# VectorE takes unit 3 between the gram products of the two batches, and the output's sums of squares behind the first two units' products

## The chip, the cores and the metric

One Trainium2 chip, one core of it. The core has TensorE (PE in the profile, PEld its weight loads), VectorE (DVE), ScalarE (ACT), GpSimd (POOL) and SyncE (SP, which only issues DMAs here). The metric is the device time in microseconds of one execution; the median of several runs is quoted. The profile is of one execution and is a little off the median.

## The reference, cut to what matters

Two sequences of 4096 rows of 512 values go through a layer norm; the result feeds two branches, whose outputs are both added to the input.

```python
xn = layernorm(x)
x  = x + attn(xn) + ffn(xn)

# attn: gated delta rule, 16 heads, keys of 16, values of 32
q, k, v = silu(causal_conv4(xn @ W))
S = S * exp(g);  delta = (v - k S) * beta;  S = S + k delta;  o = q S      # per row
o = o * rsqrt(mean(o * o over the 32 values of a head) + eps)              # sums of squares
o = o * silu(gate);  attn = o @ o_w.T

# ffn: 4-bit weights, 1408 inner columns
h = silu(xn @ gate_w.T) * (xn @ up_w.T);  y = h @ down_w.T;  ffn = y / rms(y)
```

## The kernel before, in words

The 4096 rows are taken in 32 tiles of 128 rows, both batches together (`NB = 2`). The kernel is written by hand, engine by engine: each engine has one step function (`sp_step`, `pool_step`, `act_step`, `dve_step`, `pe_step`), whose order of calls is the order of its queue, and every dependence is a wait on a semaphore. A step has two tiles: `t`, the previous one, whose attention is finished in this step, and `n`, the present one, whose projections, convolution, decay matrices, gram matrices and whole feed-forward part are made in it. There are 33 steps: the first has no `t`, the last no `n`, and 31 have both.

What the steps of the prediction touch:

- **Units.** The feed-forward part makes 22 units, `unit(0)` to `unit(21)`: even ones are a 128-column slice of gate, odd ones of up. PE makes four partial products in two halves (`half_unit`, lines 1127 to 1155), ACT copies the first one scaled into `fa` (line 613), and DVE adds the other three with their scales (`unit`, line 893). ACT takes the silu of a gate (`gate(m)`, line 624), and DVE multiplies it with the up slice (`hidden(m)`, line 905). `fa` has four slots, so ACT's copy of unit 5 waits for `hidden(1)`. PE's `down(m)` (line 1166) uses the hidden slices, and PE's units wait for earlier units of DVE to give their PSUM back.
- **Gram products.** PE makes the gram matrices of one batch (`gram(b)`, line 1354) in four PSUM banks; DVE multiplies them with the decay matrix (`gram_products(b)`, lines 987 and 988), one result going to DRAM through SP (lines 391 to 400) as the matrix that POOL solves, the other staying as `D`. The gram of batch 1 uses the same banks, so it waits for the products of batch 0. PE's transposes of v (line 1469) and its unit 5 wait for the products of batch 1.
- **The output's norm.** For the previous tile, ACT copies the output out of PSUM and squares it into `osq` (line 776), DVE sums the squares by head into `so` (line 1049), POOL makes the scale from them (lines 535 and 538, a power) and multiplies the gated output with it (`gated_and_scaled`, line 543), one instruction a batch. PE transposes the scaled output (`turn_o`, line 1366, behind unit 8), ACT copies it, and PE multiplies it with the output weights (`to_wo`, line 1376).
- **The solve.** POOL's next work, `solve` (lines 494 to 515), inverts a 32 x 32 triangle per head by 62 instructions; it first clears its result (lines 501 and 503) and waits for the DMA that brings the matrix. SP writes the result to DRAM and reads it back turned (lines 411 and 417), and PE's `t_times_r` (line 1221) uses it in the next step.

PE's order around the change is:

```python
unit(2); gram(0); unit(3); gram(1); unit(4)
# transposes of v, both batches
unit(5); unit(6); unit(7); down(0)
# then unit(8), turn_o, unit(9), down(1), unit(10), to_wo(0, 0), ...
```

Of the kernel before, what the change touches and what calls it, by code (L numbers as in the profile page):

```python
# [91 lines left out]
def build(nc, A, out):  # L92
# [4 lines left out]
    with ExitStack() as ctx:  # L97
# [258 lines left out]
        def bank(u, fill):  # L356

            return (6 if u in (1, 3) else 2 if u % 2 else 4) + fill
# [506 lines left out]
        def dve_step(eng, t, n, more):  # L865
# [15 lines left out]
            def unit(u):  # L881

                if not n:
                    return
                m = u // 2
                eng.wait_ge(*fa_scaled.at(n, u + 1))
                for k in range(1, KB):
                    if k == 2:
                        eng.wait_ge(*gu_out.at(n, 2 * u + 2))
                        eng.wait_ge(*fa_second.at(n, u + 1))  # L890
                    elif k == 3:
                        eng.wait_ge(*fa_third.at(n, u + 1))
                    eng.scalar_tensor_tensor(out=fa[:, u % 4, :], in0=PS[:, bank(u, k // 2), k % 2 * NB * P:][:, 0:NB * P],  # L893
                                             scalar=sc[:, u % 2, KB * m + k:KB * m + k + 1], in1=fa[:, u % 4, :],
                                             op0=ALU.mult, op1=ALU.add).then_inc(
                        (fa_second, fa_third, fa_done)[k - 1].sem, 1)

            def hidden(m):
                if not n:
                    return  # L900
                eng.wait_ge(*sg_done.at(n, m + 1))
                eng.wait_ge(*fa_done.at(n, 2 * m + 2))
                if m == 0:
                    eng.wait_ge(*halo_out.at(n, 1))
                eng.tensor_tensor(inner[:, m, :], fa[:, (2 * m + 1) % 4, :], sg[:, m % 2, :], ALU.mult).then_inc(h_done.sem, 1)  # L905
# [69 lines left out]
            def gram_products(b):  # L975
                if not n:
                    return
                eng.wait_ge(*gram_out.at(n, b + 1))
                eng.wait_ge(*decay_done.at(n, b + 1))

                def heads(ap):
                    return ap.rearrange("p (f g e i) -> p g f (e i)", f=NHALF, g=4, e=2)

                Gq = PS[:, 0:4, 0:4 * CH].rearrange("p g (f n) -> p g f n", f=NHALF)
                Gk = PS[:, 0:4, 4 * CH:8 * CH].rearrange("p g (f n) -> p g f n", f=NHALF)
                Eb = E[:, b, :, :].rearrange("p h i -> p (h i)")
                eng.tensor_tensor(heads(kbq[:, b, :]), Gk, heads(Eb), ALU.mult).then_inc(a_done.sem, 1)
                eng.tensor_tensor(heads(D[:, b, :, :].rearrange("p h i -> p (h i)")), Gq, heads(Eb),  # L988
                                  ALU.mult).then_inc(p_done.sem, 1)
# [53 lines left out]
            unit(1)  # L1043
            unit(2)
            gram_products(0)
            if t:
                for b in range(NB):
                    eng.wait_ge(*osq_done.at(t, b + 1))
                    eng.tensor_reduce(so[:, b, :], osq[:, b, :].rearrange("p (h v) -> p h v", v=DV), AX.X,
                                      ALU.add).then_inc(so_done.sem, 1)  # L1050
            gram_products(1)
            unit(3)
            hidden(0)
            hidden(1)
            if not n:
                result(0)
                result(1)
# [16 lines left out]
        @block.vector  # L1074
        def _(eng):
            eng.memset(eps[:, :], 1e-6).then_inc(zeroed.sem, 1)
            eng.memset(mhalf[:, :, :], -0.5).then_inc(zeroed.sem, 1)
            eng.memset(halo[:, :, :, :], 0.0).then_inc(zeroed.sem, 1)
            eng.memset(S[:, :, :, :, :], 0.0).then_inc(zeroed.sem, 1)
            first = Tile(0, 0, first=True)  # L1080
            layer_norm_stats(eng, first)
            layer_norm_apply(eng, first)
            eng.wait_ge(first_loaded.sem, 16 * 2)
            eng.wait_ge(gup_loaded.sem, 32)
            for i in range(2):
                decode(eng, i)
            eng.wait_ge(consts_loaded.sem, 16 * 11)
            eng.tensor_copy(identb[:, :], ident[:, :]).then_inc(consts_done.sem, 1)
            eng.tensor_copy(laterR[:, :], later[:, :]).then_inc(consts_done.sem, 1)
            eng.tensor_tensor(biasS[:, :], bias[:, 0, :], bias[:, 1, :], ALU.add).then_inc(consts_done.sem, 1)  # L1090
            eng.tensor_scalar(negm[:, :], tri[:, :], 1.0, 30000.0, ALU.subtract, ALU.mult).then_inc(consts_done.sem, 1)
            eng.wait_ge(alog_exp.sem, 1)
            eng.tensor_scalar(negA[:, :], negA[:, :], -1.0, None, ALU.mult).then_inc(consts_done.sem, 1)
            eng.tensor_scalar(sc[:, 0, :], sc16[:, 0, :], F8_UNIT, None, ALU.mult).then_inc(consts_done.sem, 1)
            eng.tensor_scalar(sc[:, 1, :], sc16[:, 1, :], F8_UNIT * F8_UNIT, None, ALU.mult).then_inc(consts_done.sem, 1)
            for i in range(2, KB):
                decode(eng, i)
            eng.wait_ge(dnp_loaded.sem, 32)
            for i in range(KB, len(strips)):
                decode(eng, i)  # L1100
            run(eng, dve_step)
# [458 lines left out]
```

## Time and profile before

| | |
|---|---|
| median of 3 runs | 3336.32 us (3335.82 to 3341.81) |
| the profiled execution | 3332.51 us, its span 3330.7 us |
| TensorE clock granted | 0.988 of full speed on average |
| busy share | PE 94%, DVE 72%, POOL 58%, ACT 50% |
| instructions | 118645 |

The profile's page gives busy times of engines over the span, the chain of work that ended last, and the costliest groups of instructions by source line. A timeline lists one engine's instructions in order, merged where the same line follows itself; a bracket behind a row is idle time of that engine just before it, with what ended it. All rows of timelines below are from one tile in the middle of the loop, but for those of the last tile.

### The profile page before, as it was taken

Reading aid. Unit: us, or ns where it says so; the run is one execution under the profiler, and the core shown is the slowest. Engines: PE = TensorE matmul, PEld = TensorE weight load, DVE = VectorE, ACT = ScalarE, POOL = GpSimd, SP = SyncE. Lnnn points to the kernel's source line nnn. Section 1 sums busy time; section 2 is a strip of 40 time slices with the busy share of each in tenths; the row PEclk is TensorE's granted clock in tenths of the full one; section 3 lists DMA queues with packets and bytes.
Section 4 is the critical chain, followed back from the end, with each engine's and each line's share of the span. In section 5 each row is a group of like instructions: output and inputs, shape, how many; then the busy total and the mean of one; then the engine's idle time right before and its main releaser. Section 6 shows DMA issues by size and latency. Waiting matters only on the chain.

```text
span 3330.7 us, 118645 instructions
## 1 busy us (share of the span) xinstructions
PE 3142.1 (94%) x45632; PEld 2252.9 (68%) x45632; DVE 2390.6 (72%) x5408; ACT 1667.4 (50%) x3306; POOL 1918.8 (58%) x2865
## 2 busy tenths in 40 slices
PE   5999999999999999999999999999999999999995
PEld 4666766766666766666767767667667666767663
DVE  7677776777776777777777767777767777767772
ACT  3544554544554545554445545445545455544452
POOL 4566555666555665556665556665556655556652
PEclk8999999999999999999999999999999999999996
DMA  3111111111111111111111111111111111111111
GB/s 112 39 46 27 37 43 33 46 45 28 34 43 36 46 37 27 43 37 42 46 27 37 43 33 46 46 27 37 43 33 46 40 28 39 42 37 46 34 25 30
DMA packets 318318, 132.08 MB, mean 40 GB/s; under 512 B 277089, under 2 KB 278881, under 8 KB 317793
## 3 DMA queue, kind: packets, MB, share of 16 engines
q1 hardware_dynamic: 313824, 119.26, 14.3%
q8 instruction: 383, 6.28, 0.8%
q10 hardware_dynamic: 4096, 6.42, 0.5%
q14 instruction: 15, 0.11, 0.0%
HBM read 75.30 MB, written 50.33 MB: 38 GB/s over the span
## 4 chain that ended last, share of the span: by engine, by line
PE 77%; DVE 12%; issue 6%; POOL 2%; ACT 1%; ACTq 1%; DMA 1%; DVEq 0%; SPq 0%; POOLq 0%
PE PS L1166 17%; PE PS L1122 13%; PE PS L1153 8%; PE PS L1235 7%; PE PS L1154 7%; PE PS L1376 6%; DVE arena L893 4%; PE PS L1221 3%; PE PS L1300 2%; PE PS L1253 2%; DVE arena L378 2%; PE PS L1271 2%; PE PS L1391 2%; DVE arena L988 1%; PE PS L1178 1%
## 5 line engine op out<-in xcount | busy, mean ns | idle before, releaser
L893 DVE SCALAR_TENSOR_TENSOR arena<-PS,sc,arena 128x256 f32<-128x256 f32 x2112 | 1001.0, 482 | 253.0 <-ACT arena L613 152.2
L1153 PE MATMUL PS<-xh,wgu 128*128 128x256 f32 x2816 | 871.6, 341 | 35.9 <-DVE arena L893 35.4
L613 ACT ACTIVATE arena<-PS,sc 128x256 f32<-128x256 f32 x704 | 330.0, 474 | 759.0 <-PE PS L1154 700.3
L1154 PE MATMUL PS<-xl,wgu 128*128 128x256 f32 x2816 | 698.8, 282 | 0.0
L1166 PE MATMUL PS<-wdn,inner 128*128 128x512 f32 x1408 | 650.7, 592 | 0.0
L1153 PEld LDWEIGHTS PS<-xh,wgu 128*128 128x128 f32 x2816 | 531.2, 189 | 155.8 <-issue 84.2
L511 POOL TENSOR_TENSOR work<-arena 128x31 f32<-128x31 f32 (+15 forms) x992 | 511.9, 516 | 137.5 <-DMA arena<-scr_a 62.3
L515 POOL TENSOR_TENSOR arena<-arena,work 128x31 f32<-128x31 f32 (+15 forms) x992 | 542.1, 546 | 77.7
L1154 PEld LDWEIGHTS PS<-xl,wgu 128*128 128x128 f32 x2816 | 530.4, 188 | 83.2 <-issue 83.2
L1122 PE MATMUL PS<-xnT,wqkv 128*128 128x256 f32 x2048 | 485.6, 388 | 25.2 <-ACT inner L593 15.4
L1122 PEld LDWEIGHTS PS<-xnT,wqkv 128*128 128x128 f32 x2048 | 383.6, 192 | 93.1 <-ACT inner L593 16.4
L877 DVE SCALAR_TENSOR_TENSOR qkv<-inner,cw,qkv 128x256 f32<-128x256 f32 x768 | 398.8, 557 | 55.9 <-ACT qkv L600 46.7
L1166 PEld LDWEIGHTS PS<-wdn,inner 128*128 128x128 f32 x1408 | 245.5, 189 | 199.8 <-issue 199.4
L1235 PE MATMUL PS<-wg,xnT 128*128 128x512 f32 x512 | 264.8, 621 | 0.0
L1376 PE MATMUL PS<-wo,arena 128*128 128x512 f32 x512 | 242.0, 596 | 0.0
L378 POOL TENSOR_TENSOR R<-arena,ckg 128x256 f32<-128x256 f32 x64 | 57.3, 913 | 314.1 <-DVE ckt L959 314.1
L632 ACT ACTIVATE ub<-PS 32x512 f32<-32x512 f32 x256 | 136.7, 580 | 202.2 <-PE PS L1253 197.6
L905 DVE TENSOR_TENSOR inner<-arena,sg 128x256 f32<-128x256 f32 x352 | 203.4, 585 | 30.5 <-DVE arena L893 0.5
L624 ACT ACTIVATE sg<-arena 128x256 f32<-128x256 f32 x352 | 145.2, 413 | 154.1 <-DVE arena L893 153.8
L915 DVE TENSOR_TENSOR tmp<-PS,bdmask 128x128 f32<-128x128 f32 x256 | 74.1, 289 | 206.2 <-PE PS L1271 201.8
L533 POOL TENSOR_TENSOR arena<-arena 128x512 f32<-128x512 f32 x64 | 80.4, 1278 | 226.3 <-ACT qkv L776 226.3
L1071 DVE SCALAR_TENSOR_TENSOR obuf<-PS,yr,obuf 128x512 f32<-128x512 f32 x64 | 45.1, 745 | 217.6 <-POOL yr L527 217.6
(147 smaller groups left out, 4619.2 us busy)
## 6 DMA issues: line engine op xcount, KB each, us to landing
xt<-in_x SPq DMA_DIRECT2D x64, 256.0 KB, 2.8
scr_a<-arena SPq DMA_DIRECT2D x64, 256.0 KB, 2.4
arena<-scr_a SPq DMA_DIRECT2D x256, 64.0 KB, 3.2
obuf<-in_x SPq DMA_DIRECT2D x64, 256.0 KB, 2.8
scr_t<-arena SPq DMA_DIRECT2D x32, 512.0 KB, 2.7
arena<-scr_t SPq DMA_DIRECT2D x256, 64.0 KB, 2.3
out<-obuf SPq DMA_DIRECT2D x64, 256.0 KB, 2.0
wqkv<-in_wqkv ACTq DMA_DIRECT2D x1, 2048.0 KB, 14.3
```

The lines of the kernel that those rows point to most:

```text
L511: eng.tensor_tensor(pr, la[:, j, j + 1:].unsqueeze(1).broadcast_to([P, w, r]), bc(lt[:, 0:w, j], r), ALU.mult).then_inc(solve_part.sem, 1)
L515: eng.tensor_tensor(tail, tail, pr, ALU.subtract).then_inc((t_done if j == CH - 2 else solve_part).sem, 1)
L613: eng.activation(fa[:, u % 4, :], PS[:, bank(u, 0), 0:NB * P], ACT.Copy, scale=sc[:, u % 2, KB * m:KB * m + 1]).then_inc(fa_scaled.sem, 1)
L877: eng.scalar_tensor_tensor(out=acc, in0=cin[:, mm, :, k:k + P], scalar=cw[:, mm, k:k + 1], in1=acc, op0=ALU.mult, op1=ALU.add).then_inc((t ...
L893: eng.scalar_tensor_tensor(out=fa[:, u % 4, :], in0=PS[:, bank(u, k // 2), k % 2 * NB * P:][:, 0:NB * P], scalar=sc[:, u % 2, KB * m + k:K ...
L905: eng.tensor_tensor(inner[:, m, :], fa[:, (2 * m + 1) % 4, :], sg[:, m % 2, :], ALU.mult).then_inc(h_done.sem, 1)
L1122: ins = eng.matmul(PS[:, proj_bank(m), 0:NB * P], wqkv[:, kb, m * P:(m + 1) * P], xnT[:, kb, :], start=(kb == 0), stop=(kb == KB - 1))
L1153: eng.matmul(o, w, xh[:, k, :], start=True, stop=False)
L1154: ins = eng.matmul(o, w, xl[:, k, :], start=False, stop=True)
L1166: ins = eng.matmul(PS[:, b, :], inner[:, m, b * P:(b + 1) * P], wdn[:, m, :], start=(m == 0), stop=(m == FM - 1))
L1235: ins = eng.matmul(PS[:, 4 + b, :], xnT[:, kb, b * P:(b + 1) * P], wg[:, kb, :], start=(kb == 0), stop=(kb == KB - 1))
L1376: ins = eng.matmul(PS[:, 6 + b, :], oT[b][:, kb, :], wo[:, kb, :], start=(kb == 0), stop=(kb == KB - 1))
```

## The change

In DVE's queue unit 3 and the gram products of batch 1 go ahead of the two sums of squares, unit 3 first; hidden 0 and hidden 1 follow, and the sums of squares come last. No instruction and no wait is added or removed.

```diff
             unit(1)
             unit(2)
             gram_products(0)
+            unit(3)
+            gram_products(1)
+            hidden(0)
+            hidden(1)
             if t:
                 for b in range(NB):
                     eng.wait_ge(*osq_done.at(t, b + 1))
                     eng.tensor_reduce(so[:, b, :], osq[:, b, :].rearrange("p (h v) -> p h v", v=DV), AX.X,
                                       ALU.add).then_inc(so_done.sem, 1)
-            gram_products(1)
-            unit(3)
-            hidden(0)
-            hidden(1)
             if not n:
                 result(0)
                 result(1)
```

## Rows read from the trace of the kernel before

**Rows 1.** The page, busy time of each engine.

```profile
PE 3142.1 (94%) x45632; PEld 2252.9 (68%) x45632; DVE 2390.6 (72%) x5408; ACT 1667.4 (50%) x3306; POOL 1918.8 (58%) x2865
```

**Rows 2.** Table by stretch: length, busy PE, PEld, DVE, ACT, POOL, clock, DMA.

```profile
983.00:1000.00 17.00, 14.29 (x347) 12.16 (x336) 15.87 (x34) 11.71 (x22) 9.81 (x7) 1.00 0.23 51
1000.00:1038.00 38.00, 38.00 (x177) 24.65 (x176) 28.08 (x59) 10.49 (x24) 32.31 (x57) 1.00 0.12 35
1051.00:1084.00 33.00, 32.45 (x857) 22.58 (x856) 23.35 (x59) 20.41 (x41) 12.31 (x16) 1.00 0.05 16
```

**Rows 3.** Timeline of DVE, 985 to 1000: start, length, engine, line, operation.

```profile
990.28 0.68 DVE L987 TENSOR_TENSOR arena<-PS,arena 128x512 f32<-128x512 f32 x1
...
991.48 1.27 DVE L1049 TENSOR_REDUCE so<-qkv 128x16 f32<-128x512 f32 x2
992.80 0.69 DVE L987 TENSOR_TENSOR arena<-PS,arena 128x512 f32<-128x512 f32 x1
...
994.01 1.58 DVE L893 SCALAR_TENSOR_TENSOR arena<-PS,sc,arena 128x256 f32<-128x256 f32 x3
995.51 0.75 DVE L905 TENSOR_TENSOR inner<-arena,sg 128x256 f32<-128x256 f32 x2
996.18 3.09 DVE L893 SCALAR_TENSOR_TENSOR arena<-PS,sc,arena 128x256 f32<-128x256 f32 x6
999.37 0.83 DVE L905 TENSOR_TENSOR inner<-arena,sg 128x256 f32<-128x256 f32 x1
```

**Rows 4.** What PE waited for, whole span: total us, times, longest.

```profile
PE PS L1153 <- DVE arena L893: 35.4, 97, 0.5
...
PE PS L1221 <- DMA arena<-scr_t: 10.6, 1, 10.6
```

**Rows 5.** Timeline of POOL, 992 to 1004.

```profile
992.95 0.22 POOL L535 TENSOR_SCALAR ro<-so 128x32 f32<-128x32 f32 x1 [1.10 <-DVE so L1049]
993.35 5.45 POOL L538 TENSOR_TENSOR ro<-ro,mhalf 128x32 f32<-128x32 f32 x1 [0.18 <-POOL ro L535]
998.87 2.24 POOL L543 TENSOR_TENSOR arena<-arena,ro 128x512 f32<-128x512 f32 x2
1001.05 0.95 POOL L501 MEMSET arena<- 128x1024 f32 x1
...
1003.69 0.24 POOL L511 TENSOR_TENSOR work<-arena 128x31 f32<-128x31 f32 x1 [1.38 <-DMA arena<-scr_a]
```

**Rows 6.** Timeline of PE, gram of batch 1, output transposes, unit 9.

```profile
991.71 1.06 PE L1354 MATMUL PS<-arena,kbT 32*32 32x128 f32 x64 [0.92 <-DVE arena L988]
...
1002.56 1.03 PE L1366 MATMUL PS<-ident,arena 128*128 128x128 f32 x8
1003.35 0.36 PE L1153 MATMUL PS<-xh,wgu 128*128 128x256 f32 x1
```

**Rows 7.** Timeline of ACT: copy of unit 3, gate 1, copy of unit 5.

```profile
990.36 0.47 ACT L613 ACTIVATE arena<-PS,sc 128x256 f32<-128x256 f32 x1 [0.58 <-PE PS L1154]
...
993.92 0.41 ACT L624 ACTIVATE sg<-arena 128x256 f32<-128x256 f32 x1
996.02 0.47 ACT L613 ACTIVATE arena<-PS,sc 128x256 f32<-128x256 f32 x1 [1.69 <-DVE inner L905]
```

**Rows 8.** Timelines of POOL and PE in the last tile.

```profile
3309.50 0.22 POOL L535 TENSOR_SCALAR ro<-so 128x32 f32<-128x32 f32 x1
...
3315.41 2.05 POOL L543 TENSOR_TENSOR arena<-arena,ro 128x512 f32<-128x512 f32 x2
...
3316.51 2.12 PE L1366 MATMUL PS<-ident,arena 128*128 128x128 f32 x8 [11.30 <-POOL arena L543]
```

**Rows 9.** Timelines of SP (the eight reads) and PE, 1044 to 1052.

```profile
1044.39 4.05 SPq L417 DMA_DIRECT2D arena<-scr_t  x8
...
1051.21 0.88 PE L1221 MATMUL PS<-R,arena 32*32 32x48 f32 x64
```

**Rows 10.** The page, DMA issues: count, KB each, us to landing.

```profile
arena<-scr_t SPq DMA_DIRECT2D x256, 64.0 KB, 2.3
```

## The prediction

> **What bounds the kernel now.** The page's busy line comes first: PE is busy 94% of the span, VectorE (DVE) and GpSimd (POOL) far less [rows 1]. An average can't say whether a re-ordering on DVE matters, so the next view is the table by stretch of one tile in the middle of the loop, whose pattern the other tiles repeat. In the stretch from 983 to 1000, where the change lies, DVE is busy 15.87 of 17.00 us and PE 14.29; from 1000 to 1038 PE is busy all 38.00 us [rows 2]. So in the first stretch PE waits for DVE, and in the second nothing but PE's own work sets the pace: whatever delays PE there is lost whole.
>
> The first stretch line by line: on DVE the products of batch 0 begin at 990.28, the two sums of squares at 991.48, the products of batch 1 at 992.80, unit 3 at 994.01, hidden 0 and 1 at 995.51, units 4 and 5 at 996.18, with no idle time printed between them [rows 3]. The end of unit 5 (996.18 + 3.09 = 999.27) releases PE's last matmuls of unit 7; PE's waits for unit instructions are 35.4 us in 97 waits, some 1.1 us a tile [rows 4].
>
> The sums of squares have a reader on another engine. POOL sits idle for 1.10 us until they are there, starts line 535 at 992.95, then the power of line 538 (5.45 us), then two multiplies of line 543 (2.24 us), and only then goes on to the solve [rows 5]. PE reads the result of line 543 in the transposes of line 1366, which stand behind unit 8. PE comes to them at 1002.56 and finds both finished (998.87 + 2.24 = 1001.11): no wait is printed there [rows 6]. That slack, 1002.56 - 1001.11 = 1.45 us for batch 1, is what the change spends.
>
> **The change, part by part.** No instruction is added or taken out; four groups change places on DVE. Their lengths, start to start, are [rows 3]: products 1.20 us (990.28 to 991.48) and 1.21 (992.80 to 994.01), the two sums 1.32 (991.48 to 992.80), unit 3 1.50 (994.01 to 995.51), the two hidden products 0.67 (995.51 to 996.18).
>
> Unit 3 would start at 991.48 instead of 994.01. It needs ACT's scaled copy, which ran from 990.36 for 0.47 us, to 990.83: ready [rows 7]. It ends its 1.50 us at 992.98. The products of batch 1 need PE's gram of batch 1, which runs from 991.71 for 1.06 us, to 992.77 [rows 6]: ready, so they start at 992.98, 0.18 us later than before. PE's transposes of v and then unit 5 wait for them and come 0.18 us later; DVE needs unit 5 only behind unit 4, at about 996.18 + 1.55 = 997.7, so this is covered by unit 4 on DVE. If that cover were gone it would be 0.18 x 31 = 6 us. Hidden 1 needs ACT's second gate, done at 993.92 + 0.41 = 994.33 [rows 7]; hidden 0 starts at 992.98 + 1.21 = 994.19 and hidden 1 at about 994.53: just ready. Hidden 1's earlier end serves ACT, which waited 1.69 us for it before its copy of unit 5 [rows 7]; but that copy isn't read until 997.7, so I cost the gain at nothing.
>
> The sums start at 990.28 + 1.20 + 1.50 + 1.21 + 0.67 = 994.86 instead of 991.48: **3.38 us later**. Units 4 and 5 start at 994.86 + 1.32 = 996.18, as before. DVE's sum is the same, so PE gains nothing in this stretch.
>
> Now POOL. It is waiting already, so all 3.38 us pass on: line 535 at 996.33. How fast the chain can go to PE is seen in the last tile, where PE really waits for it: 3309.50 for line 535, 3315.41 for line 543, 3316.51 for PE's transposes [rows 8]. That is 7.01 us to the first batch, so PE starts it at 996.33 + 7.01 = 1003.34 instead of 1002.56: a stall of 0.78. The second batch is ready when the pair of line 543 ends: 998.87 + 3.38 + 2.24 = 1004.49. From there to PE I take 0.07 us, the remainder in the last tile if half of the pair's 2.05 us is the first batch (3315.41 + 1.03 = 3316.44, PE at 3316.51). So PE starts batch 1 at 1004.56. Both batches took 1003.35 - 1002.56 = 0.79 us, one 0.40; unit 9 starts at 1004.96 instead of 1003.35 [rows 6]: **1.61 us lost per tile**.
>
> The multiplies of line 543 took 2.24 us beside DVE's hidden 2, which itself took 0.83 us where two hidden products take 0.75 elsewhere; in the last tile, with DVE idle, the pair took 2.05 [rows 3, 5, 8]. In the new order hidden 3 comes at about 1002.9, again beside the pair, so I take 2.24; with 2.05 the loss is 1.42. The Trainium skill (GPSIMD Engine Reference, Specifications) says that POOL's SBUF access is shared with VectorE and contends with VectorE instructions that have two SBUF inputs. By that rule the pair stays at 2.24 us and the loss is 1.61; without it, 1.42.
>
> 31 of the 33 steps hold both a previous and a present tile, where this happens; the first has no previous tile, the last no unit 3 and no products. 31 x 1.61 = 49.9 us. POOL's moved chain also leaves POOL later for the solve, which waited 1.38 us for its DMA and started at 1003.69 [rows 5]. The memset that precedes it moves from 1001.05 to 1004.43, and the solve to about 1004.43 + (1003.69 - 1.38 - 1001.05 = 1.26) + 0.1 (an estimate, from the 0.07 above) = 1005.8, 2.1 us late, 0.5 more than PE. The eight reads of its result are now issued from 1044.39 for 4.05 us and land 2.3 us after issue, the last at about 1047.9 + 2.3 = 1050.2; PE uses them at 1051.21 [rows 9, 10]. The 0.5 us fits into that 1.0 us, at nothing; without cover it would be 0.5 x 31 = 16 us. On SP's queue the write of batch 1 to DRAM waits for these products and comes at most 0.18 us later, less than the 2.1 us by which POOL itself is late for the data that come of it.
>
> The sum: 3332.5 us (the profiled execution: span 3330.7 and 1.8 around it) + 49.9 = 3382.4. The median of the runs, 3336.3, is 3.8 us above that execution; I forecast **3386 us** on the median's scale, 1.5% slower.
>
> **The rivals.** *First, slower still:* PE also waits for the solve's read-back at line 1221. For it: POOL falls 0.5 us further behind than PE. Against it: about 1.0 us of slack, and the only wait for that DMA in the trace is the last tile's [rows 4, 9]. With no slack at all it gives 3386 + 16 = 3402.
>
> *Second, no change:* the late sums are hidden because the lost PE time is won back in later waits. PE has no idle time from 1000 to 1038 and 0.55 us of 33 behind 1051 [rows 2]; all of that recovered would be 17 us (3369), so a full cover has nowhere to come from. A full cover gives 3336 and would need other PE work ahead of the transposes, and the code puts none there. The Trainium skill (Perfetto Trace Analysis, Identifying the Most-Contended Engine) would have one work on the engine with the highest occupancy, which is PE here. By that rule a POOL that is busy 58% could be late at no cost: 3336. The trace speaks against it, since PE's queue passes the point only 1.45 us behind POOL.
>
> *Third, faster:* the gain is on PE's waits for units 4 and 5 in the first stretch. If ACT, released 1.3 us earlier by hidden 1, and not DVE's queue, set the end of unit 5, and if POOL made up its lateness, the 35.4 us of PE waits would go: 3301. It decides as soon as DVE stands idle ahead of unit 5; the trace shows units 4 and 5 as one block of 3.09 us with no idle time [rows 3].
>
> **How the numbers follow.** The forecast has 0.82, the first rival 0.08, no change 0.06, faster 0.04. The range runs from 3368 (1.42 us per tile is 3380; with 0.4 us per tile won back in later waits, 12 us less) to 3404 (the first rival at full price, rounded up). A measurement of this kernel can tell about 0.2%, 6.7 us, from no change. Slower by more than that: 0.82 + 0.08 = 0.90; within it 0.06; faster 0.04.
>
> **What would show it.** In the changed kernel's trace: the sums of squares start 3.4 us later against the products of batch 0; POOL's wait ahead of line 535 grows from 1.10 to about 4.5 us a tile; PE shows waits for line 543's result of about 0.8 us twice a tile, some 50 us in all, where now there is only the last tile's; the stretch up to unit 7 keeps its length, and a tile grows by 1.6 us. I am wrong if PE shows no wait there, if units 4 and 5 start earlier against the products of batch 0, or if line 1221 begins to wait for its DMA in every tile.

## The result and the profile after

The changed kernel takes 3406.23 us (median of 3 runs, 3405.2 to 3409.62) against 3336.32: a ratio of 1.0201, 95% interval 1.0187 to 1.0215, slower by 69.9 us. The forecast was 3386, slower by 49.9; the sign and the first mechanism held, the size was short by 20 us, and the time lies 2 us above the forecast range, which ended at 3404.

The page of the changed kernel, busy times and the chain that ended last by engine. The busy line answers to [rows 1]; in the chain POOL had 2% before and PE 77%.

```profile
PE 3160.2 (93%) x45632; PEld 2254.2 (66%) x45632; DVE 2377.3 (70%) x5408; ACT 1666.4 (49%) x3306; POOL 1929.0 (57%) x2865
...
PE 57%; POOL 19%; DVE 10%; issue 8%; DMA 2%; SPq 1%; ACT 1%; POOLq 1%; ACTq 1%; DVEq 0%
```

Busy times hardly move, and POOL's busy share even falls; only the chain shows that POOL's work now stands on the path.

Timeline of DVE in one tile (start, length, engine, line), to be held against [rows 3]:

```profile
1011.37 0.68 DVE L987 TENSOR_TENSOR arena<-PS,arena 128x512 f32<-128x512 f32 x1
...
1012.56 1.58 DVE L893 SCALAR_TENSOR_TENSOR arena<-PS,sc,arena 128x256 f32<-128x256 f32 x3
1014.06 0.68 DVE L987 TENSOR_TENSOR arena<-PS,arena 128x512 f32<-128x512 f32 x1
...
1015.26 0.75 DVE L905 TENSOR_TENSOR inner<-arena,sg 128x256 f32<-128x256 f32 x2
1015.93 1.27 DVE L1053 TENSOR_REDUCE so<-qkv 128x16 f32<-128x512 f32 x2
1017.12 3.09 DVE L893 SCALAR_TENSOR_TENSOR arena<-PS,sc,arena 128x256 f32<-128x256 f32 x6
1020.30 0.42 DVE L905 TENSOR_TENSOR inner<-arena,sg 128x256 f32<-128x256 f32 x1
...
1023.84 0.81 DVE L905 TENSOR_TENSOR inner<-arena,sg 128x256 f32<-128x256 f32 x1
```

From the products of batch 0 to the sums it is 4.56 us instead of 1.20; unit 4 starts 5.75 us behind those products, against 5.90 before; the 0.15 us gain nothing, since PE then waits for POOL. Timeline of POOL in the same tile, against [rows 5]:

```profile
1017.40 0.22 POOL L535 TENSOR_SCALAR ro<-so 128x32 f32<-128x32 f32 x1 [4.45 <-DVE so L1053]
1017.80 5.44 POOL L538 TENSOR_TENSOR ro<-ro,mhalf 128x32 f32<-128x32 f32 x1 [0.18 <-POOL ro L535]
1023.32 2.24 POOL L543 TENSOR_TENSOR arena<-arena,ro 128x512 f32<-128x512 f32 x2
1025.50 0.95 POOL L501 MEMSET arena<- 128x1024 f32 x1
1026.60 0.16 POOL L503 MEMSET arena<- 128x32 f32 x1 [0.15 <-POOL arena L501]
1027.10 0.24 POOL L511 TENSOR_TENSOR work<-arena 128x31 f32<-128x31 f32 x1 [0.34 <-POOL arena L503]
```

POOL's wait for the sums has gone from 1.10 to 4.45 us, and the solve (last row) now waits for POOL's own clearing, no longer for its DMA. Timeline of PE there and at the read-back of the solve, against [rows 6, 9]:

```profile
1024.50 0.65 PE L1366 MATMUL PS<-ident,arena 128*128 128x128 f32 x4 [0.84 <-POOL arena L543]
1025.61 0.66 PE L1366 MATMUL PS<-ident,arena 128*128 128x128 f32 x4 [0.46 <-POOL arena L543]
1026.02 0.36 PE L1153 MATMUL PS<-xh,wgu 128*128 128x256 f32 x1
...
1074.37 0.88 PE L1221 MATMUL PS<-R,arena 32*32 32x48 f32 x64 [0.42 <-DMA arena<-scr_t]
...
1077.11 1.05 PE L1221 MATMUL PS<-R,arena 32*32 32x48 f32 x80
1078.39 0.71 PE L1221 MATMUL PS<-R,arena 32*32 32x48 f32 x48 [0.24 <-issue]
```

What PE waited for over the span (total us, times, longest), against [rows 4]:

```profile
PE PS L1366 <- POOL arena L543: 51.6, 63, 11.3
...
PE PS L1153 <- DVE arena L893: 20.8, 64, 0.4
...
PE PS L1221 <- DMA arena<-scr_t: 16.0, 15, 10.7
...
PE PS L1469 <- DVE arena L988: 15.7, 32, 0.5
PE PS L1221 <- issue: 14.1, 30, 1.1
```

Two rows of the same view of the kernel before, not shown so far:

```profile
PE PS L1469 <- DVE arena L988: 10.5, 32, 0.3
...
PE PS L1221 <- issue: 4.9, 13, 1.3
```

The stall at the transposes is there in every tile, as forecast, at 51.6 - 11.3 = 40.3 us (the 11.3 are the last tile's, as before) where the prediction named some 50. New beside it are waits for the read-back in 14 tiles more, and idle time inside the products of line 1221 that the profile gives to no wait ("issue"), 14.1 us where the kernel before had 4.9 in 13 times.

The tile as a whole, worked out from the timelines: the mean over 28 tiles of the time since the products of batch 0 began, in us. The columns e1 to e9 are the experiments below; e8, the control, has its figures in its own paragraph.

| | before | changed | e1 | e2 | e3 | e4 | e5 | e6 | e7 | e9 |
|---|---|---|---|---|---|---|---|---|---|---|
| sums of squares (the first) start | 1.20 | 4.56 | 4.56 | 4.56 | 4.56 | 1.20 | 3.89 | 4.56 | 4.56 | 4.56 |
| solve starts (POOL) | 13.36 | 15.73 | 15.73 | 14.15 | 14.15 | 13.57 | 14.88 | 15.73 | 14.15 | 14.52 |
| next tile's projections start (PE) | 50.43 | 52.01 | 50.29 | 52.01 | 50.30 | 50.82 | 51.14 | 52.01 | 50.30 | 50.00 |
| solve ends (POOL) | 51.08 | 53.77 | 53.46 | 51.79 | 52.00 | 51.29 | 52.88 | 53.77 | 52.01 | 52.43 |
| line 1221 starts (PE) | 60.95 | 62.84 | 62.44 | 62.52 | 60.97 | 61.33 | 61.88 | 62.75 | 60.98 | 61.52 |
| line 1221 ends | 66.93 | 69.17 | 68.71 | 68.39 | 67.32 | 67.19 | 68.27 | 68.59 | 66.81 | 67.38 |
| next tile's products of batch 0 | 100.92 | 103.34 | 102.66 | 102.42 | 101.27 | 101.14 | 102.31 | 102.57 | 100.79 | 101.55 |

The second column less the first: 1.58 us are lost at the transposes (52.01 - 50.43), 0.31 more at the start of line 1221 (1.89 - 1.58), 0.35 while it runs (6.33 against 5.98), 0.18 behind it: 2.42 us a tile. Over 31 tiles that is 75 us; the profiled executions differ by 72.7 (3405.2 - 3332.5), as the stretch ahead of the first tile's products is 2.8 us shorter and the one behind the last tile's 0.5 longer, and the medians by 69.9. POOL's solve starts 2.37 us late and ends 2.69 us late, 1.11 more than PE. In the changed kernel line 1221 starts 62.84 - 53.77 = 9.07 us behind the solve; so in the kernel before it could have started at 51.08 + 9.07 = 60.15 and did at 60.95: POOL's slack against PE was 0.80 us. In e1 and e9, where PE waits for the read-back in every tile, the step of 9.07 is 8.98 and 9.09, so the slack is 0.8 to 0.9.

### The profile page after: what moved, and what is told of

It is laid out like the page before. It is cut to its first block, busy times and chain, and to the rows that moved or that the text cites. A ratio compares the mean times of both kernels' runs of the same rounds, so it can differ in the third digit from the quotient of the medians.

```text
span 3403.4 us, 118645 instructions
## 1 busy us (share of the span) xinstructions
PE 3160.2 (93%) x45632; PEld 2254.2 (66%) x45632; DVE 2377.3 (70%) x5408; ACT 1666.4 (49%) x3306; POOL 1929.0 (57%) x2865
## 4 chain that ended last, share of the span: by engine, by line
PE 57%; POOL 19%; DVE 10%; issue 8%; DMA 2%; SPq 1%; ACT 1%; POOLq 1%; ACTq 1%; DVEq 0%
PE PS L1122 10%; PE PS L1166 10%; PE PS L1235 7%; POOL arena L515 6%; POOL work L511 6%; POOL ro L538 5%; PE PS L1153 5%; PE PS L1154 4%; PE PS L1376 4%; PE PS L1221 3%; PE PS L1300 3%; DVE arena L893 2%; PE PS L1253 2%; DVE arena L378 2%; PE PS L1271 2%
## 5 line engine op out<-in xcount | busy, mean ns | idle before, releaser
L905 DVE TENSOR_TENSOR inner<-arena,sg 128x256 f32<-128x256 f32 x352 | 183.0, 528 | 30.5 <-DVE arena L893 0.5
```

## The experiments

**Theory 1:** the late sums delay two chains, PE's transposes and, through POOL's queue, the solve with its read-back; each has its own slack and the later one sets the tile. **Theory 2:** the stall at the transposes is the loss, and the rest goes with it. Ratios are to the kernel before on the same chip in the same group of runs, which stood at 3326 us for e1 to e4, 3332 for e5 to e8 and 3337 for e9; so the ratios carry the verdicts, and the table's last row may be off by some 0.3 us a tile (10 us over 31 tiles) between groups.

**e1: the transposes one unit later.**

```diff
                 if i % 2:
                     down((i - 7) // 2)
-                elif i == 8:
-                    turn_o()
-                elif i <= 16:
+                    if i == 9:
+                        turn_o()
+                elif 10 <= i <= 16:
```

> The changed order, with TensorE's transposes of the scaled output one unit later (behind unit 9 and its down product), so that TensorE no longer stands in front of GpSimd's late multiplies. Theory 1 (two chains are late by the same cause, and the later one sets the time: TensorE at the transposes by 1.6 us a tile, GpSimd's solve and its read-back by 2.7 us of which about 0.8 was slack): the stall at the transposes goes, the wait ahead of line 1221 takes its place, and the time stays at 3395 to 3406 us. Theory 2 (the stall at the transposes is the loss, the rest is a side effect that goes with it): 1.58 us a tile come back, 3406 - 49 = 3357 us or less.

Measured: 3386.18 us, ratio 1.0179 (1.0160 to 1.0199). Theory 1 asked for 1.0176 to 1.0210 (3395 to 3406 against 3336), theory 2 for 1.0063 (3357). PE's waits, in total, and the chain that ended last:

```profile
PE PS L1221 <- DMA arena<-scr_t: 40.7, 31, 12.6
...
PE PS L1122 <- ACT inner L593: 23.2, 32, 6.8
...
PE PS L1366 <- POOL arena L543: 11.3, 1, 11.3
...
POOL 39%; PE 26%; DVE 12%; issue 12%; DMA 5%; SPq 3%; POOLq 2%; ACT 1%; ACTq 1%; DVEq 0%
```

The stall at the transposes is gone in all tiles but the last, PE begins the next projections at 50.29, earlier than before the change, and gives more than half of it back (the tile is 0.68 us shorter, not 1.72): it waits for the read-back in every tile (40.7 - 12.6 = 28.1 us) and for ACT's copies of the projections, which stand behind POOL's late scale of the feed-forward output. The second chain is enough by itself to make the kernel 1.8% slower.

**e2: POOL clears the solve's result ahead of the output's norm.**

```diff
                 keys_for_state(eng, t, n)
+            if n:
+                clear(eng, n)
             if t:
                 gated_and_scaled(eng, t)
```

(`clear` holds the waits and the two clearing instructions of lines 496 to 503, taken out of `solve`, which still comes behind `gated_and_scaled`.)

> The changed order, with GpSimd clearing the solve's result (lines 501 and 503) ahead of the output's norm instead of behind it. Theory 1: the solve starts about 1.2 us earlier, GpSimd's lateness falls from 2.7 to about 1.5 us, less than TensorE's own 1.6, so the waits ahead of line 1221 go and the stall at the transposes remains: 3336 + 31 x 1.58 = 3385 us. Theory 2: no change, 3406 us.

Measured: 3377.45 us, ratio 1.0145 (1.0124 to 1.0167); theory 1 asked for 3385 / 3336 = 1.0147, theory 2 for no change, 1.0201. PE's waits:

```profile
PE PS L1371 <- POOL arena L546: 51.7, 63, 11.3
...
PE PS L1226 <- DMA arena<-scr_t: 9.3, 1, 9.3
```

(Lines are shifted by 5 on PE, by 3 on POOL.) With the solve 1.58 us earlier the read-back waits go but for the last tile's, line 1221 takes 5.87 us again, and the unchanged stall at the transposes is all that remains: 102.42 - 100.92 = 1.50 us a tile. This is the term that the prediction had.

**e3: both edits.**

> The changed order with both edits, the transposes later and the clearing earlier. Theory 1: GpSimd is late by about 1.5 us against a slack of 0.8, TensorE has no stall at the transposes: 0.5 to 0.8 us a tile remain, 3352 to 3361 us. Theory 2: the same as with the transposes later alone, 3336 to 3357 us.

Measured: 3343.73 us, ratio 1.0055 (1.0037 to 1.0072), inside theory 1's 1.0048 to 1.0075, but inside theory 2's 1.0000 to 1.0063 too, so this time alone does not tell them apart. The three runs together do: neither edit alone brought back more than 0.6%, both together bring back 1.5%: two chains side by side, as theory 1 has it. Line 1221 starts as in the kernel before (60.97), but still takes 6.35 us.

**e4: only unit 3 goes ahead of the products of batch 1.**

The edit is to the kernel before:

```diff
+            unit(3)
             gram_products(1)
-            unit(3)
             hidden(0)
             hidden(1)
```

> Only the first half of the change: unit 3 ahead of the products of batch 1, the sums of squares kept behind the products of batch 0. Theories 1 and 2 alike: the sums are on time, the order of the rest costs nothing, 3336 us within 7. A rival, that the products of batch 1 coming 1.5 us later (unit 3 stands ahead of them with the sums) delay TensorE's transposes of v and unit 5: some 1 us a tile, 3367 us.

Measured: 3343.94 us, ratio 1.0055 (1.0036 to 1.0074): neither of the two. PE's waits:

```profile
PE PS L1469 <- DVE arena L988: 52.1, 32, 1.7
...
PE PS L1153 <- DVE arena L893: 7.7, 28, 0.3
```

Both the sums and unit 3 now stand ahead of the products of batch 1. PE's transposes of v wait 1.63 us a tile for them instead of 0.33 [10.5 us in 32 before], and its waits for units fall from 35.4 to 7.7 us: 1.30 more against 0.89 less, 0.41 a tile. Not all of the loss is the order's: in five of the tiles the granted clock falls from 1.00 to 0.50 (2.4 to 1.2 GHz) for 3.4 us, 0.1 to 0.5 us behind the end of that longer wait. PE's timeline and the table by stretch in one of them (length, busy PE, PEld, DVE, ACT, POOL, clock, DMA):

```profile
491.69 1.88 PE L1469 MATMUL PS<-ident,qkv 128*128 128x128 f32 x8 [1.68 <-DVE arena L988]
...
491.78:495.18 3.40, 3.40 (x17) 3.40 (x18) 2.00 (x6) 0.72 (x2) 3.32 (x2) 0.50 0.54 108
```

There the next projections come at 51.4 to 51.8 us, in the other tiles at 50.65, 0.22 later than before the change; without the five the mean tile is 101.02 us. No other profiled execution has such a fall between 200 and 3200 us; why the clock falls in these five alone was not tried. So the half of the change that moves unit 3 is not free unless the sums leave that place; the two halves need each other.

**e5: the sums ahead of hidden 0 and 1.**

```diff
             gram_products(1)
-            hidden(0)
-            hidden(1)
             if t:
                 ...
+            hidden(0)
+            hidden(1)
```

> The changed order, but the sums of squares ahead of hidden 0 and 1 instead of behind them: the sums come 2.71 us later than before the change instead of 3.38. Theory 1 (each chain has its own slack, and the later one sets the time): TensorE's stall at the transposes falls from 1.58 to 0.9 us a tile, GpSimd's solve is late by 1.7 to 2.0 us, 0.8 to 1.1 more than TensorE, which its slack of 0.8 nearly covers; 0.9 to 1.5 us a tile remain, 28 to 47 us above the kernel before. Rival (the loss follows the delay in proportion): 2.42 x 2.71 / 3.38 = 1.94 us a tile, 60 us above the kernel before.

Measured: 3373.89 us, ratio 1.0130 (1.0113 to 1.0147), 42 us above the kernel before: inside theory 1's range, and the proportional 60 us is outside the interval. The sums start 0.67 us earlier than in the changed kernel; PE's projections come 0.87 earlier and line 1221 0.96.

**e6 and e7: SyncE's load of x earlier.** In the changed kernel this load is issued right behind the eight reads of the solve, 1074.37 - 1072.80 = 1.57 us ahead of line 1221; in the kernel before it was 1051.21 - 1049.21 = 2.00. Timelines of SP, the changed kernel and the kernel before:

```profile
1072.80 0.91 SPq L389 DMA_DIRECT2D xt<-in_x  x2
...
1049.21 0.91 SPq L389 DMA_DIRECT2D xt<-in_x  x2
```

It goes ahead of SyncE's wait for the solve, a tile earlier in the loop (SyncE's loop is taken apart at its ends for that); e6 does that to the changed kernel, e7 to e3.

```diff
-            if more:
-                ...
+            if n and not t:
+                load_x(n)
...
+            if more:
+                load_x(n.next())
             hold(eng, *t_done.at(n, 1))
```

> The changed order, with SyncE's load of the next rows of x issued some 10 us earlier, ahead of its wait for the solve, so that it no longer runs beside TensorE's products of line 1221. Theory 1 (the 0.35 us by which these products last longer, idle time that the profile gives to no wait, comes from the load beside them): that time goes, 11 us less than the changed kernel, ratio to before 1.017. Rival (it comes from elsewhere, the late read-back itself or the order): 1.020, unchanged.

> The changed order with the transposes later, the clearing earlier and the load of x earlier. Theory 1: the 0.35 us a tile that the version without the earlier load still lost go too, and the time is that of the kernel before within 0.2%. Rival: unchanged at 1.0055 times the kernel before.

Measured: e6 3388.34 us, ratio 1.0176 (1.0159 to 1.0193); e7 3335.88 us, ratio 1.0008 (0.9998 to 1.0018). PE's waits in e6 (lines shifted by 10):

```profile
PE PS L1231 <- DMA arena<-scr_t: 13.3, 8, 10.9
...
PE PS L1231 <- issue: 4.0, 17, 0.7
```

The idle time without a wait falls from 14.1 to 4.0 us, line 1221 takes 5.84 us in e6 and 5.83 in e7. By the table e6 is 0.77 us a tile shorter than the changed kernel: 0.49 at line 1221, 0.19 behind it, 0.09 ahead of it. Its ratio alone is not clear of the changed kernel's (1.0187 to 1.0215); that of e7 is clear of e3's. With all three edits the changed order is within 0.1% of the order before, so these three places hold nearly all of its loss of 2.0%. The comparison of like with like is e7 against e8 below, which has the same load in the order before: 3335.88 against 3327.56 us, ten runs each, so 0.2% are left without a place. The profiled execution of e7 was its fastest (3329.0 us), so its trace cannot show where.

**e8: the load of x earlier in the kernel before, the control.**

> The kernel before with the load of x earlier and nothing else, the control. Theory 1: in the kernel before the load comes mostly behind the products of line 1221 or beside few of them, 0 to 3 us less than before, the same within 0.2%. Rival (the load costs the kernel before as much): 11 us less, ratio 0.997.

Measured: 3327.56 us, ratio 0.9993 (0.9983 to 1.0002): the same. In its trace line 1221 takes 66.82 - 60.99 = 5.83 us instead of 5.98, and the tile 100.78 instead of 100.92. So beside these products the load costs 0.15 us a tile where the read-back comes in time, and 0.5 (6.33 against 5.84) where it, and with it the load, comes late against PE.

**e9: the norm split by batch,** on top of e7, a try at a version that beats both: batch 0's sum behind hidden 1, batch 1's behind unit 5, and a power and a multiply on POOL for each batch.

```diff
             hidden(1)
-            if t:
-                ...
+            sums(0)
...
                 unit(2 * m + 1)
+                if m == 2:
+                    sums(1)
                 hidden(m)
```

> The version with the transposes later, the clearing and the load of x earlier, and the output's norm split by batch: VectorE sums the squares of batch 0 behind hidden 1 and those of batch 1 only behind unit 5, and GpSimd makes the scale of each batch by itself. Theory 1 (up to unit 7 TensorE is paced by VectorE's queue, and what stands behind unit 5 is free): units 4 and 5 come 0.66 us earlier, TensorE's remaining 20.8 us of waits for units go, GpSimd's two shorter powers (2.9 us each, an estimate from 5.44 us at 32 columns and 0.72 at 2) end no later than the one did: 0.5 us a tile, 15 us less, 0.996 times the kernel before. Rival (the split makes GpSimd's chain longer, and the read-back is late again): the same as the kernel before or slower, 1.000 to 1.010.

Measured: 3356.07 us, ratio 1.0064 (1.0050 to 1.0078): the rival. Timeline of POOL in one tile:

```profile
1005.06 0.20 POOL L549 TENSOR_SCALAR ro<-so 128x16 f32<-128x16 f32 x1 [3.86 <-DVE so L926]
1005.45 2.92 POOL L552 TENSOR_TENSOR ro<-ro,mhalf 128x16 f32<-128x16 f32 x1 [0.18 <-POOL ro L549]
1008.44 1.26 POOL L556 TENSOR_TENSOR arena<-arena,ro 128x512 f32<-128x512 f32 x1
1009.78 0.20 POOL L549 TENSOR_SCALAR ro<-so 128x16 f32<-128x16 f32 x1
1010.17 2.90 POOL L552 TENSOR_TENSOR ro<-ro,mhalf 128x16 f32<-128x16 f32 x1 [0.18 <-POOL ro L549]
1013.15 1.05 POOL L556 TENSOR_TENSOR arena<-arena,ro 128x512 f32<-128x512 f32 x1
```

The powers took 2.9 us each as estimated, but the two rounds end 0.37 us later (solve at 14.52 against 14.15), and PE comes 0.30 us earlier as hoped (50.00 against 50.30). That opens the gap on the read-back by 0.67 us, and line 1221 starts 0.54 us later than in e7. No version here beats the kernel before by more than the noise.

## Why the prediction was right and where it was short

**DVE's queue: right.** The sums came 3.36 us later (forecast 3.38), POOL's wait for them is 4.45 us (4.5), unit 4 starts where it did, within 0.15 us. The cover of the products of batch 1 held too: PE's waits at line 1469 grew by 5.2 us in all (15.7 - 10.5), those for units fell by 14.6.

**The stall at the transposes: right.** Unit 9 and all behind it come 1.58 us later, forecast 1.61; e2 shows that term by itself as a ratio of 1.0145, which on 3336 us is 48 us (forecast 49.9). The profile prints 0.84 + 0.46 = 1.30 us of idle time for it, less than the delay, since the ends of matmuls are modelled and the row ahead of each of the two waits runs some 0.2 us into it.

**The solve and its read-back: the step that failed.** The prediction said that the solve is 2.1 us late, 0.5 more than PE, and that "The 0.5 us fits into that 1.0 us, at nothing". It measured 2.69 us late at its end, 1.11 more than PE, against a slack of 0.80. Three things were mis-sized: the step from the clearing to the solve, taken at 0.1 us, measured 0.34; the solve itself, taken as unchanged, lasts 38.04 us instead of 37.72 (53.77 - 15.73 against 51.08 - 13.36); and the slack, taken at 1.0, was 0.80. The excess is 0.31 us a tile at line 1221, 10 us in all. The prediction's own sign of this, a wait of line 1221 for its DMA, is printed in 14 tiles more, not in every one. The first rival, priced at 16 us for no slack, is thus in part what happened, on top of the forecast.

**Line 1221 lasting longer: not foreseen.** 0.35 us a tile; e6 and e7 show that it goes when the load of x is issued elsewhere, e8 that the load costs 0.15 us there where the read-back is on time. How the load does it is open: the profile names no wait there. The last 0.18 us lies in the products of line 1300 and beyond, where idle time without a wait grew from 12.1 to 16.0 us; it is gone in e6 (68.59 to 102.57, 33.98 us as in the kernel before), but in e1 too (33.95), where the load stayed, so its cause is open.

**The two rules.** POOL's multiplies took 2.24 us for the pair beside hidden 3, which took 0.81 us where hidden 2, ahead of the pair, took 0.42: for these multiplies the trace agrees with the Trainium skill (GPSIMD Engine Reference, Specifications) as the prediction used it. The Trainium skill's rule on the engine with the highest occupancy (Perfetto Trace Analysis, Identifying the Most-Contended Engine) names the engine to work on first; that a less busy one may be late at no cost was the prediction's own step to its second rival, and it fails here. In e1 POOL, busy 57% of the span, has 39% of the chain that ended last, and PE, busy 93%, has 26%.

## What to carry to other kernels

Before an instruction is moved back in one engine's queue, list who reads its result and what stands behind that reader in its own queue; a reader that already waits passes the whole delay on, and each consumer has a slack of its own. Compare the slacks against each other as well as against zero: here the second chain had 0.8 us, and mending either chain alone brought back at most 0.6% of 2.0%. A slack of less than 1 us should be priced as used up when the estimates in front of it are tenths of a microsecond wide.

## What the runs showed of the hardware

When a DVE product with two SBUF inputs (line 905) meets a two-input product of POOL, one of the two pays: the one that starts later. In the changed kernel DVE's row at 1023.84 took 0.81 us beside line 543; the pair below fell together at 1039.7, and there DVE, which had started first, took its usual 0.42 while POOL took 0.89. Timelines of POOL and DVE in that tile; the means over 29 tiles of this solve instruction are 0.90 us here and 0.70 in the kernel before, where the meeting falls elsewhere in each tile.

```profile
1039.74 0.89 POOL L515 TENSOR_TENSOR arena<-arena,work 128x240 f32<-128x240 f32 x1
...
1039.65 0.42 DVE L905 TENSOR_TENSOR inner<-arena,sg 128x256 f32<-128x256 f32 x1
```

A count over the changed kernel's trace, with POOL's products of lines 511, 515 and 543: of the 352 products of line 905, 135 started with more than 0.15 us of a running POOL product left and ended 0.28 us behind its end, while POOL's took no more than 0.02 us over its shortest; 47 started ahead of a POOL product, took 0.43 us, and that one took 0.19 to 0.23 us more than its shortest. Beside POOL's power (line 538, two inputs of 32 columns) DVE paid nothing: the product at 1020.30 lies inside the power of 1017.80 to 1023.24 and took 0.42 us.

The solve is longer by 0.32 us because its instructions last longer (33.25 us of busy time instead of 32.93), not because it waits. The meetings are at the same places of every tile in the changed kernel (hidden 6 starts 12.55 to 12.56 us behind the solve's start) and wander in the kernel before (12.80 to 13.70). That they are the whole of the 0.32 us was not tested: the solve lasts 37.64 us in e2, 37.73 in e1, where POOL and PE are bound to each other in every tile, and 37.98 in e8.

A power on POOL costs by its columns: 0.72 us at 128 x 2 (line 527), 2.9 at 128 x 16, 5.44 at 128 x 32.
